# Self attention with its head mixing in two column halves and its value and score weights on two row halves

## The chip, the cores and the metric

The kernel runs on one core of a Trainium2 chip. The metric is the time of one execution on the device, in microseconds (us). TensorE (PE in the profile) multiplies matrices, VectorE (DVE), ScalarE (ACT) and GpSimd (POOL) work on elements, SyncE (SP) issues the transfers. Each engine runs its own instructions in order and waits on semaphores for the others.

## The reference

A perceiver block: cross attention, self attention and a feed forward part, each added to `x`, which has 64 sequences of 32 rows of 512. The change touches self attention alone:

```python
def _holo_linear(x, basis, phase, amp):
    resonance = jnp.einsum('bsd,hd->bsh', x, basis)      # 512 -> 64
    w = amp * jnp.cos(phase)                             # 512 x 64
    return jnp.einsum('bsh,oh->bso', resonance, w)
q = _holo_linear(hidden_states, basis_q, phase_q, amp_q)   # k and v alike
# 16 heads of 32
scores = jnp.einsum('bhqd,bhkd->bhqk', q, k) * scale
attn = jax.nn.softmax(scores, axis=-1)
out = jnp.einsum('bhqk,bhkd->bhqd', attn, v)
# heads side by side: 512
return _holo_linear(out, basis_o, phase_o, amp_o)
...
x = x + _L0_attn_ref(_layernorm(x, axis=-1), ...)
```

## The kernel before

`perceiver_block` runs one stage after another, each in a block of its own: `query_path`, `cross_attention`, `root_deviations`, `holo_weights`, `self_attention`, `root_deviations` again, `fold_weights` and `feed_forward`. A block ends when all engines are through it.

`holo_weights` loads amplitudes, phases and bases, forms amplitude times cosine and multiplies them into `score_w` (64 rows, per head 64 columns) and `value_w` (per head 64 columns, kept on partitions 64 to 127). `out_w` (64 rows of 512) are the output weights. The unused halves of `phase` and `amp` are cleared by VectorE (L1079, L1080), and SyncE waits for that ahead of the two loads of the output weights (L1069, L1072).

`self_attention` goes through 16 tiles of 128 rows, that is four sequences each. All data is fp32, for which TensorE executes each matmul as two passes; a transpose is one pass. A tile `t` takes these steps on TensorE, each with the engine that takes its result out of PSUM:

- `turn_input` (L1218): four transposes of the normalised rows, which GpSimd makes one to two tiles ahead (L1207, L1209); ScalarE copies them to `xn_t` (L1353).
- `reduce_input` (L1227): 8 matmuls with the bases; ScalarE copies `reduced` (L1362; queries' part on partitions 0 to 63, values' part on 64 to 127) and twice `keys` (L1365).
- `score_weights` (L1238): 8 matmuls of 128 columns, on rows 0 to 63; ScalarE copies one half to `u_sb` (L1377), VectorE the other (L1340).
- `score` (L1249): 8 matmuls of 64 columns. VectorE takes the peak (L1304) and subtracts it (L1306), ScalarE takes the exponential (L1385), VectorE sums (L1311), inverts (L1313) and scales (L1315).
- `turn_weights` (L1265): four transposes of the weights; VectorE and ScalarE copy two blocks each to the block-diagonal `e_t` (L1181).
- `value_weights` (L1257): 2 matmuls of 512 columns, on rows 64 to 127; VectorE (L1329) and ScalarE (L1357) copy half each to `z_sb`.
- `mix` (L1273): 16 matmuls, one for each head, with 64 stationary columns, all adding into one 64 x 128 area; ScalarE copies it to `ro_sb` (L1381).
- `project` (L1278): 1 matmul of 512 columns, on rows 0 to 63. VectorE adds it to the rows of `x` (L1322) and forms the negative mean (L1325), ScalarE sums the squares (L1370), VectorE stores both (L1335, L1336).

The order of the steps is written out by hand and spans three tiles. On TensorE a step of the loop is:

```python
turn_input(t, v); project(t - 2); value_weights(t - 1, 1 - v)
reduce_input(t, v); turn_weights(t - 1, 1 - v)
score_weights(t, v); mix(t - 1); score(t, v)
```

Queries for one tile are weighed while the tile before is mixed. Turned weights and projection share a PSUM bank (`P_BANK`), so `turn_weights` waits for VectorE's addition; the mix shares the bank of the reduction. SyncE issues the loads of `fold_weights` at the start of the stage (`loads.first`).

Elsewhere in the kernel, `reduce` of the query path (L432) writes alternating matmuls to two column halves:

```python
for ab in range(2):
    one = nc.tensor.matmul(ps[ab * R:(ab + 1) * R, QR_BANK, s * B:(s + 1) * B], m_sb[:, ab, sign, at * R:(at + 1) * R],
                           q_sb[:, ab, sign, s * B:(s + 1) * B], start=True, stop=True)
```

Of the kernel before, what the change touches and what calls it, by code (L numbers as in the profile page):

```python
# [1047 lines left out]
def holo_weights(nc, amp_nat, phase_nat, basis_t, basis_o, amp_o, phase_o, half_pi, basis, score_w, value_w, out_w):  # L1048
# [3 lines left out]
    with ExitStack() as ctx:  # L1052
# [8 lines left out]
        loaded, cleared, stepped, cosined, weighed, multiplied, kept = (  # L1061
            sem(f"h_{n}") for n in ("loaded", "cleared", "stepped", "cosined", "weighed", "multiplied", "kept"))
        block = ctx.enter_context(nc.Block())

        @block.sync
        def _(sp):
            sp.dma_start(phase[:, 0:NAT], phase_nat.rearrange("p t i -> p (t i)")).then_inc(loaded, 16)
            sp.wait_ge(cleared, 1)
            sp.dma_start(phase[0:HARM, NAT:], phase_o).then_inc(loaded, 16)  # L1069
            sp.dma_start(amp[:, 0:NAT], amp_nat.rearrange("p t i -> p (t i)")).then_inc(loaded, 16)  # L1070
            sp.wait_ge(cleared, 2)
            sp.dma_start(amp[0:HARM, NAT:], amp_o).then_inc(loaded, 16)  # L1072
            sp.dma_start(bo[:], basis_o).then_inc(loaded, 16)
            sp.dma_start(basis[:], basis_t).then_inc(loaded, 16)
            sp.wait_ge(loaded, 96)

        @block.vector
        def _(dve):
            nc.vector.memset(phase[:, NAT:], 0.0).then_inc(cleared, 1)  # L1079
            nc.vector.memset(amp[:, NAT:], 0.0).then_inc(cleared, 1)  # L1080
            dve.wait_ge(loaded, 96)
            dve.wait_ge(cleared, 2)
# [12 lines left out]
            nc.vector.tensor_copy(out_w[:], amp[0:HARM, NAT:])  # L1095
# [40 lines left out]
def self_attention(nc, x1, stat, basis, score_w, value_w, out_w, ident, loads):  # L1136
# [4 lines left out]

    with ExitStack() as ctx:
# [8 lines left out]
        shifted = sb("d_shifted", [P, 2, HH, S])  # L1151
# [4 lines left out]
        ro_sb = sb("d_ro", [HARM, P])  # L1156
# [27 lines left out]
        def in_steps(engine, step):  # L1184

            step(0, 0, mid=False, old=False)
            step(1, 1, old=False)
            with engine.Fori(1, TURNS) as i:
                step(2 * i, 0)
                step(2 * i + 1, 1)  # L1190
            step(TILES, 0, new=False)
            step(TILES + 1, 1, new=False, mid=False)
# [20 lines left out]
        def _(pe):  # L1213
# [7 lines left out]
            def reduce_input(t, v):  # L1221
                pe.wait_ge(turned_out, t + 1)
                wait(pe, reduced_out, t)
                wait(pe, ro_out, t - 1)
# [27 lines left out]

            def value_weights(t, v):
                wait(pe, z_out_a, t)
                wait(pe, z_out_d, t)
                for g in range(2):
                    last = nc.tensor.matmul(ps[:, Z_BANK + g], reduced[HARM:2 * HARM, v],  # L1257
                                            value_w[HARM:2 * HARM, 8 * g:8 * g + 8].rearrange("p h j -> p (h j)"), start=True, stop=True)
                last.then_inc(z_done, 1)
# [40 lines left out]
        def _(dve):  # L1300
            def shift(t, v):
# [4 lines left out]
                nc.vector.tensor_tensor(shifted[:, v], scores, peak[:, v].unsqueeze(2).to_broadcast([P, HH, S]),  # L1306
# [10 lines left out]
            def step(t, v, new=True, mid=True, old=True):  # L1317
                if mid:
                    weigh(t - 1, 1 - v)
                if old:  # L1320
                    dve.wait_ge(out_done, t - 1)
                    nc.vector.scalar_tensor_tensor(row_of(t - 2), ps[:, P_BANK], 1.0, row_of(t - 2), ALU.mult, ALU.add,  # L1322
                                                   accum_out=row_sum[:]).then_inc(added, 1)
                    dve.wait_ge(added, t - 1)
                    nc.vector.tensor_scalar(neg_mean[:], row_sum[:], -1.0 / D, None, ALU.mult).then_inc(centred, 1)  # L1325
                if mid:
                    dve.wait_ge(z_done, t)
                    wait(dve, ro_done, t - 1)
                    nc.vector.tensor_copy(z_sb[:, 0:8].rearrange("p h j -> p (h j)"), ps[:, Z_BANK]).then_inc(z_out_d, 1)  # L1329
                if mid:  # L1330
                    dve.wait_ge(e_turned, t)
                    copy_blocks("dve", (0, 1)).then_inc(e_out_d, 1)
                if old:
                    dve.wait_ge(squared, t - 1)
                    nc.vector.tensor_copy(stat[:, 0, bass.ds(t - 2, 1)], neg_mean[:])  # L1335
                    nc.vector.tensor_copy(stat[:, 1, bass.ds(t - 2, 1)], squares[:]).then_inc(kept, 1)  # L1336
                if new:
                    dve.wait_ge(u_done, t + 1)
                    wait(dve, scored, t)
                    nc.vector.tensor_copy(u_sb[:, 1], ps[:, U_BANK + 1].rearrange("p (k b s) -> p b k s", k=HG, b=BT)).then_inc(u_out_d, 1)  # L1340
                    shift(t, v)

            dve.sem_inc(kept, 1)
            dve.wait_ge(cleared, 1)
            in_steps(dve, step)

        @block.scalar
        def _(act):
            def step(t, v, new=True, mid=True, old=True):
                if new:  # L1350
                    act.wait_ge(turned, t + 1)
                    wait(act, reduced_done, t)
                    nc.scalar.activation(xn_t[:], ps[:, T_BANK].rearrange("p (c x) -> p c x", c=CD), ACT.Copy).then_inc(turned_out, 1)  # L1353
                if mid:
                    act.wait_ge(z_done, t)
                    wait(act, ro_done, t - 1)
                    nc.scalar.activation(z_sb[:, 8:16].rearrange("p h j -> p (h j)"), ps[:, Z_BANK + 1], ACT.Copy).then_inc(z_out_a, 1)  # L1357
                if new:
                    act.wait_ge(reduced_done, t + 1)
                    wait(act, scored, t - 1)  # L1360
                    wait(act, z_done, t - 1)
                    nc.scalar.activation(reduced[:, v], ps[:, R_BANK, 0:P], ACT.Copy)  # L1362
                    for parity in range(2):
                        at = slice(parity * HARM, (parity + 1) * HARM)
                        last_key = nc.scalar.activation(keys[at, v, :, parity], ps[at, R_BANK, P:2 * P].rearrange("p (b s) -> p b s", b=BT), ACT.Copy)  # L1365
                    last_key.then_inc(reduced_out, 1)
                if old:
                    act.wait_ge(centred, t - 1)
                    act.wait_ge(kept, t - 1)
                    nc.scalar.activation(scratch[:], row_of(t - 2), ACT.Square, bias=neg_mean[:], accum_out=squares[:]).then_inc(squared, 1)  # L1370
                if mid:
                    act.wait_ge(e_turned, t)
                    copy_blocks("act", (2, 3)).then_inc(e_out_a, 1)
                if new:
                    act.wait_ge(u_done, t + 1)
                    wait(act, scored, t)
                    nc.scalar.activation(u_sb[:, 0], ps[:, U_BANK].rearrange("p (k b s) -> p b k s", k=HG, b=BT), ACT.Copy).then_inc(u_out_a, 1)  # L1377
                if mid:
                    act.wait_ge(ro_done, t)
                    wait(act, out_done, t - 1)  # L1380
                    nc.scalar.activation(ro_sb[:], ps[0:HARM, R_BANK, 2 * P:3 * P], ACT.Copy).then_inc(ro_out, 1)  # L1381
                if new:
                    act.wait_ge(shifted_out, t + 1)
                    wait(act, e_turned, t - 1)
                    nc.scalar.activation(e[:, v], shifted[:, v], ACT.Exp).then_inc(exped, 1)  # L1385

            act.wait_ge(cleared, 2)
            in_steps(act, step)


# [498 lines left out]
def perceiver_block(nc, x, x_s, cache_t, early, w_qr, w_kr, late, angle_q, centre_q, rope_kv, amp_nat, phase_nat, basis_t, basis_o, amp_o, phase_o,  # L1889
# [4 lines left out]
    with ExitStack() as ctx:  # L1894
# [27 lines left out]
        with ExitStack() as fold_scope:  # L1922
            loads = FoldLoads(nc, fold_scope, paths, ent_in, ent_out, path, columns)
            with ExitStack() as scope:
                basis, score_w, value_w, out_w = (scope.enter_context(nc.sbuf_tensor(n, shape, F32)) for n, shape in (
                    ("basis", [P, CD, 2 * P]), ("score_w", [HARM, 16, HARM]), ("value_w", [P, 16, HARM]), ("out_w", [HARM, D])))
# [71 lines left out]
```

## Time and profile before

| | before |
|---|---|
| median of 3 runs | 1765.01 us (1761.34 to 1765.61) |
| the profiled execution | 1764.15 us, span 1762.3 us |
| TensorE busy | 1547.7 us (88%) |
| VectorE busy | 1127.6 us (64%) |
| ScalarE busy | 810.1 us (46%) |
| GpSimd busy | 542.6 us (31%) |
| granted TensorE clock, mean | 0.943 |

The span runs from the first to the last instruction. Busy times are sums of instructions, of which several of TensorE can overlap; a row of a timeline can merge several instructions of one kind (their number stands behind the x). The shape of a matmul is given as rows x columns of the stationary operand, then output and input. A granted clock of 1.00 is 2.4 GHz, 0.50 is 1.2 GHz.

### The profile page before, as it was taken

What the parts mean: (1) busy time and instruction counts of PE and PEld (TensorE: products, weight loads), DVE (VectorE), ACT (ScalarE), POOL (GpSimd) and SP (SyncE); (2) the same over time, 40 slices, a digit from 0 to 9 for tenths busy, and PEclk for the clock granted to TensorE, in tenths of its full rate; (3) what the DMA queues carried; (4) which work ended last, traced back from release to release, by engine and by line L of the source; (5) the groups of instructions that cost most, each with busy time, mean ns of one, the idle gap of its engine ahead of it and who ended that gap; (6) DMA issues with size and microseconds to landing.
All of it is one profiled execution on the core that took longest, in us unless ns stands there. A gap on an engine that the chain in (4) does not pass through costs nothing. (4 is left out here: it accounts for less than half of the span.)

```text
span 1762.3 us, 26302 instructions
## 1 busy us (share of the span) xinstructions
PE 1547.7 (88%) x8136; PEld 1171.3 (66%) x8136; DVE 1127.6 (64%) x1818; ACT 810.1 (46%) x1723; POOL 542.6 (31%) x594
## 2 busy tenths in 40 slices
PE   5899999999559999999999399999758679898996
PEld 4577777777347777777777277787423258686775
DVE  6888887777257788877777224544356625464646
ACT  4565656565335555555554223433201244555553
POOL 5233443230144545455553121110041030403102
PEclk9899999999789999999999679999889879999998
DMA  4143233333384444454442130000143100000000
GB/s 159 42 123 97 88 108 109 108 100 110 103 277 110 120 110 119 114 119 113 116 113 60 54 130 0 0 0 0 72 191 140 51 0 1 25 1 24 0 25 24
DMA packets 137878, 143.46 MB, mean 81 GB/s; under 512 B 83168, under 2 KB 102752, under 8 KB 134112
## 3 DMA queue, kind: packets, MB, share of 16 engines
q1 hardware_dynamic: 136096, 133.60, 25.9%
q10 hardware_dynamic: 1728, 9.20, 1.6%
q8 instruction: 27, 0.44, 0.1%
q14 instruction: 27, 0.22, 0.0%
HBM read 113.27 MB, written 29.49 MB: 81 GB/s over the span
## 5 line engine op out<-in xcount | busy, mean ns | idle before, releaser
L901 ACT ACTIVATE c_e_t_high<-c_et_ps 128x512 fp32r<-128x512 f32 x128 | 76.7, 599 | 226.3 <-PE c_et_ps L966 226.3
L77 DVE TENSOR_TENSOR b_rot_parts_low<-b_rot,b_rot_parts_high 128x1536 fp32r<-128x1536 f32 x64 | 136.3, 2130 | 22.3 <-ACT b_rot_parts_high L526 22.3
L794 POOL TENSOR_TENSOR c_mixed_low<-c_whole,c_mixed_high 128x512 fp32r<-128x512 f32 x64 | 95.3, 1490 | 176.0 <-ACT c_mixed_high L913 176.0
L958 PE MATMUL c_sc_ps<-c_kv_t,c_q 128*128 128x257 f32 x512 | 136.3, 390 | 13.7 <-DMA c_q<-carried_queries 13.7
L1500 PE MATMUL f_ps<-f_right,f_left 128*128 128x512 f32 x256 | 115.9, 615 | 27.9 <-DMA f_right<-ent_out 20.6
L817 DVE TENSOR_REDUCE c_peak<-c_sc_ps 128x2 f32<-128x514 f32 x128 | 88.6, 692 | 54.5 <-PE c_sc_ps L958 53.8
L70 PE MATMUL e_mm_ps<-folded_high,e_h_t_high 128*128 128x512 f32 x256 | 108.7, 425 | 15.8 <-DVE e_h_t_low L77 15.7
L958 PEld LDWEIGHTS c_sc_ps<-c_kv_t,c_q 128*128 128x128 f32 x512 | 99.4, 195 | 32.9 <-DMA c_q<-carried_queries 14.5
L264 POOL TENSOR_TENSOR b_turned_raw<-b_turn_part 128x384 f32<-128x384 f32 x32 | 68.9, 2155 | 164.9 <-DVE b_key_parts_low L77 163.6
L309 DVE TENSOR_TENSOR b_rot<-b_w_qr,b_angle 128x1536 f32<-128x1536 f32 x64 | 118.9, 1858 | 0.2
L893 ACT ACTIVATE c_e<-c_sc_ps,c_peak 128x257 f32<-128x257 f32 x256 | 118.8, 475 | 0.0
L966 PE MATMUL c_et_ps<-ident,c_e 128*128 128x128 f32 x512 | 82.5, 285 | 36.8 <-DVE c_e L824 35.0
L70 PE MATMUL b_ps<-b_x_t_high,b_wq_parts_high 128*128 128x512 f32 x256 | 108.2, 423 | 5.0 <-DVE b_x_t_low L77 5.0
L1500 PEld LDWEIGHTS f_ps<-f_right,f_left 128*128 128x128 f32 x256 | 50.2, 198 | 93.7 <-issue 65.6
L70 PE MATMUL c_out_ps<-c_w_vo_high,c_mixed_high 128*128 128x512 f32 x256 | 110.7, 432 | 1.6 <-POOL c_mixed_low L794 1.6
L77 DVE TENSOR_TENSOR c_e_t_low<-c_et_ps,c_e_t_high 128x512 fp32r<-128x512 f32 x128 | 88.0, 688 | 30.4 <-ACT c_e_t_high L901 30.4
L966 PEld LDWEIGHTS c_et_ps<-ident,c_e 128*128 128x128 f32 x512 | 59.9, 144 | 71.0 <-DVE c_e L824 64.8
L260 POOL TENSOR_TENSOR b_turn_part<-b_early,b_centre 128x384 f32<-128x384 f32 x64 | 84.9, 1346 | 71.9 <-DMA b_early<-early 70.2
L526 ACT ACTIVATE b_rot_parts_high<-b_rot 128x1536 fp32r<-128x1536 f32 x64 | 95.2, 1487 | 25.3 <-PE b_ps L72 17.0
L1684 POOL TENSOR_TENSOR e_y<-e_y,out_norm 128x512 f32<-128x512 f32 x16 | 22.5, 1406 | 263.7 <-DVE e_y L1844 263.7
L72 PE MATMUL e_mm_ps<-folded_high,e_h_t_low 128*128 128x512 f32 x256 | 103.5, 404 | 0.0
L71 PE MATMUL e_mm_ps<-folded_low,e_h_t_high 128*128 128x512 f32 x256 | 103.5, 404 | 0.0
(214 smaller groups left out, 4026.2 us busy)
## 6 DMA issues: line engine op xcount, KB each, us to landing
c_q<-carried_queries SPq DMA_DIRECT2D x64, 256.0 KB, 3.6
c_ends_spread<-end_weights SPq DMA_DIRECT2D x64, 256.0 KB, 4.3
carried_queries<-x SPq DMA_DIRECT2D x7, 2048.0 KB, 11.2
b_early<-early SPq DMA_DIRECT2D x15, 640.0 KB, 3.9
c_raw<-cache_t SPq DMA_DIRECT2D x64, 128.5 KB, 3.9
c_swapped<-cache_t SPq DMA_DIRECT2D x128, 64.2 KB, 3.8
f_left<-ent_in SPq DMA_DIRECT2D x8, 1024.0 KB, 5.1
f_right<-ent_out SPq DMA_DIRECT2D x8, 1024.0 KB, 7.8
```

What stands on the lines that cost most here:

```text
L70: nc.tensor.matmul(out, left[0], right[0], start=start, stop=False)
L71: nc.tensor.matmul(out, left[0], right[1], start=False, stop=False)
L72: return nc.tensor.matmul(out, left[1], right[0], start=False, stop=stop)
L77: return nc.vector.tensor_tensor(low, value, high.bitcast(F32), ALU.subtract)
L309: nc.vector.tensor_tensor(rot[:, k % 2], weight, angles, ALU.mult).then_inc(rot_ready, 1)
L526: nc.scalar.activation(rot_parts[0][:, k % 2], rot[:, k % 2], ACT.Copy).then_inc(rot_rounded, 1)
L794: nc.gpsimd.tensor_tensor(mixed[1][:, w, :, u], whole[:, u % 2].rearrange("p (h s) -> p h s", h=H), mixed[0][:, w, :, u].bitcast(F32), ALU ...
L817: nc.vector.tensor_reduce(peak[:, v], sc_ps[:, 2 * v:2 * v + 2, 0:L], AX_X, ALU.max, negate=True).then_inc(peaked, 1)
L893: last = nc.scalar.activation(e[:, v, c], sc_ps[:, 2 * v + c, 0:L], ACT.Exp, bias=peak[:, v, c:c + 1], accum_out=total[:, v, c:c + 1])
L958: last = nc.tensor.matmul(sc_ps[:, 2 * half + c, 0:L], q[:, u, at], kv_t[:, u], start=True, stop=True)
L966: last = nc.tensor.transpose(et_ps[:, (2 * k + c) * P:(2 * k + c + 1) * P], e[:, half, c, k * P:(k + 1) * P], ident[:])
L1500: last = nc.tensor.matmul(ps[:, m], left[:, slot, m * P:(m + 1) * P], right[:, slot], start=k == 0, stop=k == CF - 1)
```

## The change

- The mix writes even heads to partitions 0 to 63 and odd heads to 64 to 127 of `P_BANK`, as two sums. `ro_sb` gets 128 rows, and `out_w` holds its 64 rows twice, so that the projection over 128 rows adds the two sums. For this `amp_o` and `phase_o` are handed over with their rows doubled; the two memsets and the waits for them go.
- `score_weights` and `value_weights` become one step, `weigh_reduced`, of the tile itself: value matmul of a half, four score matmuls of the half, and the same for the other half.
- A step of the loop has a new order, on all engines. TensorE turns and reduces the input of the next tile in it, and projects in the same step in which it mixes. `score` waits for each half of `u_sb` by itself. `shifted` has one buffer in place of two. The loop is one step shorter.

```diff
-            nc.vector.memset(phase[:, NAT:], 0.0).then_inc(cleared, 1)
-            nc.vector.memset(amp[:, NAT:], 0.0).then_inc(cleared, 1)
...
-            nc.vector.tensor_copy(out_w[:], amp[0:HARM, NAT:])
+            nc.vector.tensor_copy(out_w[:], amp[:, NAT:])
...
-        ro_sb = sb("d_ro", [HARM, P])
+        ro_sb = sb("d_ro", [P, P])
...
-            def score_weights(t, v):
+            def weigh_reduced(t, v):
+
                 pe.wait_ge(reduced_out, t + 1)
                 wait(pe, u_out_a, t)
                 wait(pe, u_out_d, t)
+                wait(pe, z_out_a, t)
+                wait(pe, z_out_d, t)
                 for g in range(2):
+                    values = nc.tensor.matmul(ps[:, Z_BANK + g], reduced[HARM:2 * HARM, v],
+                                              value_w[HARM:2 * HARM, 8 * g:8 * g + 8].rearrange("p h j -> p (h j)"), start=True, stop=True)
                     for k in range(HG):
                         h = 8 * g + 2 * k
                         last = nc.tensor.matmul(ps[:, U_BANK + g, k * P:(k + 1) * P], score_w[:, h:h + 2].rearrange("p h j -> p (h j)"),
                                                 reduced[0:HARM, v], start=True, stop=True)
-                last.then_inc(u_done, 1)
+                    last.then_inc(u_done, 1)
+                    values.then_inc(z_done, 1)
...
             def score(t, v):
-                pe.wait_ge(u_out_a, t + 1)
-                pe.wait_ge(u_out_d, t + 1)
                 wait(pe, shifted_out, t)
                 out = ps[:, S_BANK].rearrange("p (g q b s) -> p g b q s", g=2, q=2, b=BT)
                 for g in range(2):
+                    pe.wait_ge(u_out_d if g else u_out_a, t + 1)
...
                 for h in range(HH):
-                    last = nc.tensor.matmul(ps[0:HARM, R_BANK, 2 * P:3 * P], z_sb[:, h], e_t[:, h], start=h == 0, stop=h == HH - 1)
-                last.then_inc(ro_done, 1)
+                    half = h % 2
+                    one = nc.tensor.matmul(ps[half * HARM:(half + 1) * HARM, P_BANK, 0:P], z_sb[:, h], e_t[:, h],
+                                           start=h < 2, stop=h >= HH - 2)
+                    if h >= HH - 2:
+                        one.then_inc(ro_done, 1)
...
-            def step(t, v, new=True, mid=True, old=True):
+            def step(t, v, new=True, mid=True, old=True, ahead=True):
                 if new:
-                    turn_input(t, v)
-                if old:
-                    project(t - 2)
-                if mid:
-                    value_weights(t - 1, 1 - v)
-                if new:
-                    reduce_input(t, v)
+                    weigh_reduced(t, v)
                 if mid:
                     turn_weights(t - 1, 1 - v)
                 if new:
-                    score_weights(t, v)
+                    score(t, v)
+                if ahead:
+                    turn_input(t + 1, 1 - v)
                 if mid:
                     mix(t - 1)
-                if new:
-                    score(t, v)
+                if ahead:
+                    reduce_input(t + 1, 1 - v)
+                if mid:
+                    project(t - 1)
+
+            turn_input(0, 0)
+            reduce_input(0, 0)
             in_steps(pe, step)
```

VectorE's order in a step is then: `add(t - 2)` (addition and mean), copy of the score weights' second half, its two blocks of `e_t`, `keep(t - 2)`, peak and shift of `t`, sum, inverse and scaling of `t`, copy of its half of `z_sb`. ScalarE's: copy of the score weights' first half, squares of `t - 2`, its two blocks of `e_t`, copy of the input of `t + 1`, exponential of `t`, copy of the mix of `t - 1`, its half of `z_sb`, `reduced` and `keys` of `t + 1`.

## Rows read from the trace of the kernel before

**Rows 1.** The page's first line
```profile
span 1762.3 us, 26302 instructions
```

**Rows 2.** Three stretches: length, busy PE, PEld, DVE, ACT, POOL, clock, DMA, GB/s
```profile
1014.00:1027.00 13.00, 10.26 (x44) 9.30 (x44) 0.69 (x1) 3.18 (x6) 4.26 (x5) 0.50 0.98 417
...
1126.00:1159.20 33.20, 31.46 (x230) 25.54 (x228) 18.73 (x41) 14.52 (x34) 6.25 (x6) 1.00 0.00 0
...
1231.00:1248.00 17.00, 10.33 (x45) 7.74 (x44) 7.04 (x18) 4.19 (x9) 0.00 (x0) 0.78 0.00 1
```

**Rows 3.** Timeline of TensorE, one step: start, duration, instruction, [idle before]
```profile
1125.23 0.60 PE L1218 MATMUL d_ps<-ident,d_xn 128*128 128x128 f32 x4
1125.76 0.69 PE L1278 MATMUL d_ps<-out_w,d_ro 64*128 64x512 f32 x1
1125.77 0.69 PE L1257 MATMUL d_ps<-value_w,d_reduced 64*128 64x512 f32 x1
1126.30 0.59 PE L1278 MATMUL d_ps<-out_w,d_ro 64*128 64x512 f32 x1
1126.30 1.45 PE L1257 MATMUL d_ps<-value_w,d_reduced 64*128 64x512 f32 x3
1128.05 2.05 PE L1227 MATMUL d_ps<-d_xn_t,basis 128*128 128x128 f32 x16 [0.30 <-ACT d_xn_t L1353]
1130.00 0.63 PE L1265 MATMUL d_ps<-ident,d_e 128*128 128x128 f32 x4
1130.90 2.05 PE L1238 MATMUL d_ps<-d_reduced,score_w 64*128 64x128 f32 x16 [0.28 <-ACT d_keys L1365]
1132.96 3.71 PE L1273 MATMUL d_ps<-d_e_t,d_z 128*64 128x128 f32 x32
1136.60 2.00 PE L1249 MATMUL d_ps<-d_keys,d_u 128*128 128x64 f32 x16
1138.43 0.61 PE L1218 MATMUL d_ps<-ident,d_xn 128*128 128x128 f32 x4
```

**Rows 4.** Timelines of VectorE and ScalarE in the same step
```profile
1125.43 0.69 DVE L1304 TENSOR_REDUCE d_peak<-d_ps 128x16 f32<-128x512 f32 x1 [4.95 <-PE d_ps L1249]
...
1128.55 0.69 DVE L1315 TENSOR_TENSOR d_e<-d_e,d_inverse 128x512 f32<-128x512 f32 x1
...
1130.66 1.38 DVE L1181 COPY d_e_t<-d_ps 32x512 f32<-32x512 f32 x2
...
1130.14 0.28 ACT L1362 ACTIVATE d_reduced<-d_ps 128x128 f32<-128x128 f32 x1 [1.65 <-PE d_ps L1227]
1130.31 0.54 ACT L1365 ACTIVATE d_keys<-d_ps 64x128 f32<-64x128 f32 x2
```

**Rows 5.** Timeline of TensorE in the query path, around one run of line 432
```profile
301.94 0.39 PE L71 MATMUL b_ps<-b_rot_parts_low,b_key_parts_high 128*128 128x512 f32 x1
302.17 0.39 PE L72 MATMUL b_ps<-b_rot_parts_high,b_key_parts_low 128*128 128x512 f32 x1
302.48 1.15 PE L432 MATMUL b_ps<-x 128*64 128x64 f32 x32
303.56 0.50 PE L70 MATMUL b_ps<-b_x_t_high,b_wq_parts_high 128*128 128x512 f32 x1
```

**Rows 6.** Timelines, stage's start, third turn of the input, last mix, last instruction
```profile
1014.23 1.11 PE L1218 MATMUL d_ps<-ident,d_xn 128*128 128x128 f32 x4 [6.17 <-POOL d_xn L1209]
...
1046.01 0.61 PE L1218 MATMUL d_ps<-ident,d_xn 128*128 128x128 f32 x4
...
1237.77 6.66 PE L1273 MATMUL d_ps<-d_e_t,d_z 128*64 128x128 f32 x32 [1.53 <-ACT d_e_t L1181]
...
1247.79 0.14 DVE L1336 COPY stat<-d_squares 128x1 f32<-128x1 f32 x1
```

**Rows 7.** Timeline of the preparation: first memset and second load
```profile
987.39 0.48 DVE L1079 MEMSET h_phase<- 128x512 f32 x1 [0.68 <-PEq L1025]
987.90 0.47 SPq L1069 DMA_DIRECT2D h_phase<-phase_o  x1
```

More of the change, by code:

```diff
@@ L1187, in in_steps @@
             step(1, 1, old=False)
-            with engine.Fori(1, TURNS) as i:
+            with engine.Fori(1, TURNS - 1) as i:
                 step(2 * i, 0)
                 step(2 * i + 1, 1)
-            step(TILES, 0, new=False)
-            step(TILES + 1, 1, new=False, mid=False)
+            step(TILES - 2, 0)
+            step(TILES - 1, 1, ahead=False)
+            step(TILES, 0, new=False, ahead=False)
         @block.sync
@@ L1223, in reduce_input @@
                 wait(pe, reduced_out, t)
-                wait(pe, ro_out, t - 1)
                 for m in range(2):
@@ L1251, in score @@
                 last.then_inc(scored, 1)
[L1253 to L1259, printed above, removed]
             def turn_weights(t, v):
@@ L1305, in shift @@
                 dve.wait_ge(peaked, t + 1)
-                nc.vector.tensor_tensor(shifted[:, v], scores, peak[:, v].unsqueeze(2).to_broadcast([P, HH, S]),
+                wait(dve, exped, t)
+                nc.vector.tensor_tensor(shifted[:], scores, peak[:, v].unsqueeze(2).to_broadcast([P, HH, S]),
                                         ALU.subtract).then_inc(shifted_out, 1)
@@ L1315, in weigh, with step @@
                 nc.vector.tensor_tensor(e[:, v], e[:, v], inverse[:, v].unsqueeze(2).to_broadcast([P, HH, S]), ALU.mult).then_inc(weighed, 1)
-            def step(t, v, new=True, mid=True, old=True):
-                if mid:
-                    weigh(t - 1, 1 - v)
+            def step(t, v, new=True, mid=True, old=True, ahead=True):
                 if old:
[L1321 to L1329, printed above, removed]
+                    add(t - 2)
+                if new:
+                    dve.wait_ge(u_done, 2 * t + 2)
+                    wait(dve, scored, t)
+                    nc.vector.tensor_copy(u_sb[:, 1], ps[:, U_BANK + 1].rearrange("p (k b s) -> p b k s", k=HG, b=BT)).then_inc(u_out_d, 1)
@@ L1343, in _, with keep @@
+            def keep(t):
+                dve.wait_ge(squared, t + 1)
+                nc.vector.tensor_copy(stat[:, 0, bass.ds(t, 1)], neg_mean[:])
+                nc.vector.tensor_copy(stat[:, 1, bass.ds(t, 1)], squares[:]).then_inc(kept, 1)
             dve.sem_inc(kept, 1)
@@ L1345, in _ @@
             in_steps(dve, step)
+            add(TILES - 1)
+            keep(TILES - 1)
         @block.scalar
         def _(act):
-            def step(t, v, new=True, mid=True, old=True):
-                if new:
[L1351 to L1366, printed above, removed]
@@ new lines, in take_input, with take_reduced @@
+            def take_input(t):
+                act.wait_ge(turned, t + 1)
+                wait(act, reduced_done, t)
+                nc.scalar.activation(xn_t[:], ps[:, T_BANK].rearrange("p (c x) -> p c x", c=CD), ACT.Copy).then_inc(turned_out, 1)
+            def take_reduced(t, v):
+                act.wait_ge(reduced_done, t + 1)
+                wait(act, scored, t - 1)
+                nc.scalar.activation(reduced[:, v], ps[:, R_BANK, 0:P], ACT.Copy)
+                for parity in range(2):
+                    at = slice(parity * HARM, (parity + 1) * HARM)
+                    last_key = nc.scalar.activation(keys[at, v, :, parity], ps[at, R_BANK, P:2 * P].rearrange("p (b s) -> p b s", b=BT), ACT.Copy)
+                last_key.then_inc(reduced_out, 1)
@@ new lines, in square, with step @@
+            def square(t):
+                act.wait_ge(centred, t + 1)
+                act.wait_ge(kept, t + 1)
+                nc.scalar.activation(scratch[:], row_of(t), ACT.Square, bias=neg_mean[:], accum_out=squares[:]).then_inc(squared, 1)
+            def step(t, v, new=True, mid=True, old=True, ahead=True):
+                if new:
+                    act.wait_ge(u_done, 2 * t + 1)
+                    wait(act, scored, t)
+                    nc.scalar.activation(u_sb[:, 0], ps[:, U_BANK].rearrange("p (k b s) -> p b k s", k=HG, b=BT), ACT.Copy).then_inc(u_out_a, 1)
@@ L1367, in step @@
                 if old:
-                    act.wait_ge(centred, t - 1)
-                    act.wait_ge(kept, t - 1)
-                    nc.scalar.activation(scratch[:], row_of(t - 2), ACT.Square, bias=neg_mean[:], accum_out=squares[:]).then_inc(squared, 1)
+                    square(t - 2)
                 if mid:
                     act.wait_ge(e_turned, t)
+                    wait(act, ro_done, 2 * t - 2)
                     copy_blocks("act", (2, 3)).then_inc(e_out_a, 1)
[L1374 to L1381, printed above, removed]
+                if ahead:
+                    take_input(t + 1)
                 if new:
@@ L1384, in step @@
                     wait(act, e_turned, t - 1)
-                    nc.scalar.activation(e[:, v], shifted[:, v], ACT.Exp).then_inc(exped, 1)
+                    nc.scalar.activation(e[:, v], shifted[:], ACT.Exp).then_inc(exped, 1)
+                if mid:
+                    act.wait_ge(ro_done, 2 * t)
+                    wait(act, out_done, t - 1)
+                    nc.scalar.activation(ro_sb[:], ps[:, P_BANK, 0:P], ACT.Copy).then_inc(ro_out, 1)
+                if new:
+                    act.wait_ge(z_done, 2 * t + 2)
+                    wait(act, ro_done, 2 * t)
+                    nc.scalar.activation(z_sb[:, 8:16].rearrange("p h j -> p (h j)"), ps[:, Z_BANK + 1], ACT.Copy).then_inc(z_out_a, 1)
+                if ahead:
+                    take_reduced(t + 1, 1 - v)
             act.wait_ge(cleared, 2)
+            take_input(0)
+            take_reduced(0, 0)
             in_steps(act, step)
+            square(TILES - 1)
 LAYERS, PW, QUARTERS = 2, 2, 4
```

35 lines of the change are left out of this document (19 added, 16 removed).

## The prediction

> **What bounds the kernel now.** I read the page first: the profiled execution spans 1762.3 us [rows 1] and took 1764.15 us, 1.85 us more outside the span, and so lies 0.9 us under the median of 1765.01 us. The change touches two stages, so I cut the span by time. Self attention issues its first TensorE instruction at 1014.2 us and its last VectorE instruction ends at 1247.9 us [rows 6]: 233.7 us, 13% of the span, for 16 tiles. In the busy times by stretch the reader is to see that TensorE works 31.5 of 33.2 us in the middle, VectorE 18.7, ScalarE 14.5 and GpSimd 6.3, at the full granted clock [rows 2]. So TensorE bounds the stage, and what counts is the start-to-start time of its groups.
>
> The timeline of TensorE over one step gives these [rows 3]. From one turn of the input (1125.23) to the next (1138.43) are 13.20 us: turn of the input 0.53; projection and value weights up to the reduction 2.29, of which 0.30 is waiting for ScalarE; reduction 1.95; turn of the weights 0.90, of which 0.28 is waiting for the keys; score weights 2.06; mix 3.64; scores 1.83. Two kinds of rate stand in it. The mix is 32 passes (an fp32 matmul is two) in 3.64 us, 114 ns a pass. The scores are 16 passes of half as many columns, and also 114 ns each.
>
> **The change part by part, per step.**
>
> *Mix in two column halves.* The same 32 passes go, but even heads write partitions 0 to 63 and odd heads 64 to 127. The stage of before has no such pair, but line 432 of the query path has: 32 passes, 64 stationary columns, full 128 rows, output alternating between the two halves. It takes 1.08 us from its start to the next group's start [rows 5], some 0.1 us of which is the change of shape (its first pass starts 0.31 us after the matmul ahead of it, where such matmuls follow each other at 0.23). That is 31 ns a pass for 64 columns. If the mix's 114 ns at 128 columns stands for streaming, 64 columns take 57 ns; the halves therefore overlap completely there. Bounds for the mix: 3.64 us (no overlap) and 32 x 57 ns = 1.82 us; I take 1.82 + 0.10 = 1.92, by the nearest row. Gain 1.72.
> The Trainium skill, page "TensorE: Matmul & The Clock Gate", Part 3, says that a weight load overlaps a running matmul only when the row groups differ. Here both halves use all rows, so by it each pass would pay its load too, and the mix would keep a good part of its 3.64 us. Line 432 has the same shape and ran at 31 ns a pass, so the trace does not agree, and I go by the row.
>
> *Value and score weights on two row halves.* Value weights (4 passes of 512, rows 64 to 127) now go in between the score weights (16 passes of 128, rows 0 to 63): value group, eight score passes, value group, eight score passes. Today the value weights hide the projection in the same way: the first value pass starts 0.01 us after the first projection pass and 0.53 us before the second one [rows 3]. A pass of 512 takes 0.43 us (three in 1.45, the end of the last included), and the six passes need 1.99 us (1125.76 to 1127.75), not 2.6. So row halves overlap, and a pass of one half goes ahead of a waiting pass of the other. Alone the score weights take 2.06 and the four value passes 4 x 0.43 = 1.72. Bounds: 2.06 (shorter wholly inside longer) and 3.78 (one after the other). I take 2.06: the pattern is that of the projection and value pair, only with unequal lengths.
> The same part of that page states that matmuls start strictly in program order. By it the first score pass would start with the second value pass, 0.43 us late, twice a step; that is the in-order rival below. The value pass that starts before the second projection pass [rows 3] speaks against it.
>
> *Projection.* With both column halves of the mix as 128 rows and the output weights doubled, it is again two passes of 512, but on all rows, so nothing lies beside it: 2 x 0.43 = 0.86. It is moved behind the reduction, where it covers ScalarE's copies of reduced and keys. Today from the reduction's end (1130.00) to the score weights (1130.90) are 0.90 us: ScalarE starts at 1130.14, its last key copy ends at 1130.85 [rows 4]. So reduction to next step costs the larger of 0.86 and 0.90: 0.90. Without this cover the cost would be 0.86 + 0.90.
>
> *Sum.* Weights 2.06 + turn of the weights 0.55 + scores 1.83 + turn of the input 0.54 + mix 1.92 + reduction 1.95 + 0.90 = 9.75 us, against 13.20: 3.45 us a step.
>
> *Are the other engines early enough?* Count from the start of the value/score weights. ScalarE's copy of the first half of the score weights starts near 1.0 us, when eight passes are through; VectorE's of the second near 2.1, and ends at 2.8; the second half of the scores wants it at 3.5. The turned weights are there at 2.6; VectorE's two copies of 0.69 end at 4.2, ScalarE's before that; the mix starts at 4.97, as the turn of the input stands ahead of it. Scores end at 4.43. From there VectorE takes 0.20 to start and 3.8 more through peak, shift, exp, sum and scaling (1125.43 to 1129.24, [rows 4]); shift waits for nothing, since exp of the tile before is long over. ScalarE's copy of the turned input (4.97 to 5.7) is over when exp comes, near 6.1. The weights are ready near 8.5 and turned at 11.9 in the next step: 3.4 us to spare. ScalarE copies the mix near 7.0; the projection starts at 8.85. The addition for the tile before follows the projection (9.9 to 10.7), and the next turn of the weights waits for it at 11.9: 1.2 us to spare, the narrowest. VectorE is busy 18.7 and ScalarE 14.5 us in 33.2 us [rows 2], which is 7.4 and 5.8 a step, both under 9.75. GpSimd's two operations are done one tile ahead. No wait but the 0.04 in the 0.90 should be left.
>
> *Head.* In the first 24 us the granted clock is half (0.50 in 1014 to 1027, [rows 2]) and a turn of the input takes 1.11 instead of 0.60 us [rows 3, 6]. I leave the clock as it was, full from 1038 on. By the doubled terms the new order runs: input turned and reduced 14.2 to 20.7 with ScalarE, weights(0) to 24.5, scores(0) to 28.2, turn(1), 0.75 of waiting, reduction(1) to 33.7, 0.9, weights(1) to 38.3, then at full clock the rest of step 1, 8.1 us: step 2 begins at 1046.4. Today step 2 begins at 1046.0 [rows 6], so nothing is gained here: the reduction and turn of tile 2 already lie behind.
> *Middle.* 13 steps: 13 x 13.20 = 171.6 becomes 13 x 9.75 = 126.8, to 1173.2.
> *Tail.* Today 1217.6 to 1247.9, 30.3 us. New: the last full step ends with project(14) at 7.7 us; VectorE then finishes weights(15), the z copy and the addition at 9.9; turn 0.6, copies 1.5, mix 1.9, copy 0.4, projection 1.0, addition, square and store 2.1 make 17.4. TensorE has gaps of some 2 us here; today in such gaps the clock fell and the last mix took 6.66 instead of 3.71 us [rows 3, 6], so I add 1.6: 19.0. The end is at 1192.2 instead of 1247.9: 55.7 us less.
>
> *Preparation.* Two memsets go. Today the second load is issued at 987.90, right behind the end of the first memset (987.39 + 0.48, [rows 7]); it can go at once. In return two loads have 128 rows, not 64. That is at best the 0.48 of a memset gained, and I allow as much lost; I take 0. The copy of the output weights has more partitions, not more elements in each. All after the stage is moved, not changed.
>
> Sum: 1764.15 - 55.7 = 1708.5, and with the 0.9 to the median 1709.4; I say 1710.
>
> **Rivals.**
> *In-order starts.* Score passes wait for the second value pass: 0.43 + eight passes (0.91), twice, is 2.7 us, with the 0.2 of the two changes of shape 2.85 instead of 2.06. 0.8 x 16 = 12.6: 1722. With no row overlap at all 3.78, 1.72 x 16 = 27.5: 1737. For: today's pair has equal lengths, an unequal pair is nowhere in the trace.
> *Column halves don't pay.* The mix stays at 3.64: 1.72 x 16: 1737. Against it is line 432 alone. If neither overlap comes, the step is 9.75 + 1.72 + 1.72 = 13.19 us: no change, 1765. That is the rival that the change does not do what it says.
> *A new wait.* The 1.2 us of the addition or the ScalarE chain (input copy, exp, mix copy, z copy, reduced) goes by 1 us: 10.7 a step, 1725.
> *Slower: the clock.* If TensorE, with 3.5 us less streaming a step, is held at half clock, its terms grow as the last mix did (6.66 against 3.71, by 1.8): 8.85 x 1.8 + 0.9 = 16.8, 7.1 more a step. It decides against the change when more than 3.45 / 7.1, about half of the steps, run so; with all of them 1710 + 114 = 1824. Against: the clock was full throughout with 0.58 us of waiting in each step, and less is left. A later rise at the start costs 0.45 us for each us.
>
> **How the numbers follow.** Chances: the forecast 0.62 (its own range 1703 to 1719: 9.4 to 10.2 us a step and the clock's rise up to 6 us later), in-order or no row overlap 0.15, new wait 0.10, column halves 0.05, neither 0.04, clock 0.04. 1700 to 1733 takes in the first three but for their far ends. 0.3% is 5.3 us, about what a measurement tells from no change: faster 0.92, same 0.04, slower 0.04.
>
> **What would show it.** Mix 1.9 us from start to next group, starts of the two halves together; value and score passes mixed in time, 2.1 us; projection behind the reduction with under 0.1 us idle; turns of the input 9.75 us apart; the granted clock 1.00. Wrong would be: score passes that start 0.43 us late, gaps ahead of the turn of the weights with VectorE's addition as releaser, or half clock.

## The result, and the profile after

| | before | after |
|---|---|---|
| median | 1765.31 us (4 runs) | 1702.02 us (4 runs, 1701.08 to 1703.14) |
| ratio | | 0.9646, 95% interval 0.9629 to 0.9663 |
| self attention, first turn of the input to last store | 233.7 us | 170.6 us |
| a step in the middle | 13.20 us | 9.50 us |

63 us less, where 55 were forecast (1710); the range of 1700 to 1733 holds it. All of it lies in self attention: outside of the stage the profiled executions take 1528.6 us before and 1528.7 us after. One of the six executions of the kernel with neither edit (below) took 3657 us, twice as long as its others, and is left out of its numbers. The page of the kernel after, its first lines:

```profile
span 1699.3 us, 26369 instructions
## 1 busy us (share of the span) xinstructions
PE 1490.1 (88%) x8136; PEld 1129.8 (66%) x8136; DVE 1126.8 (66%) x1816; ACT 809.9 (48%) x1723; POOL 540.8 (32%) x594
```

Not one pass fewer (8136), and still less TensorE time: the busy time is no sum, as the section on the time before has it, but counts overlapping instructions once (below, 123.60 us of 123.60). The timeline of TensorE over one step (after), beside [rows 3]:

```profile
1109.77 0.69 PE L1235 MATMUL d_ps<-value_w,d_reduced 64*128 64x512 f32 x1
1109.77 0.71 PE L1239 MATMUL d_ps<-d_reduced,score_w 64*128 64x128 f32 x4
1110.30 0.59 PE L1235 MATMUL d_ps<-value_w,d_reduced 64*128 64x512 f32 x1
1110.32 0.61 PE L1239 MATMUL d_ps<-d_reduced,score_w 64*128 64x128 f32 x4
...
1111.16 0.59 PE L1235 MATMUL d_ps<-value_w,d_reduced 64*128 64x512 f32 x1
1111.21 0.61 PE L1239 MATMUL d_ps<-d_reduced,score_w 64*128 64x128 f32 x4
1111.75 0.66 PE L1258 MATMUL d_ps<-ident,d_e 128*128 128x128 f32 x4
1112.24 1.90 PE L1250 MATMUL d_ps<-d_keys,d_u 128*128 128x64 f32 x16
1113.98 0.61 PE L1215 MATMUL d_ps<-ident,d_xn 128*128 128x128 f32 x4
1114.52 1.97 PE L1267 MATMUL d_ps<-d_e_t,d_z 128*64 128x128 f32 x32
1116.41 2.05 PE L1223 MATMUL d_ps<-d_xn_t,basis 128*128 128x128 f32 x16
1118.30 1.02 PE L1274 MATMUL d_ps<-out_w,d_ro 128*128 128x512 f32 x2
1119.27 0.69 PE L1235 MATMUL d_ps<-value_w,d_reduced 64*128 64x512 f32 x1
```

Each value pass has four score passes beside it, and the 32 passes of the mix take 1.89 us, 59 ns each in place of 114. The mean of a pass, 59 ns, includes the start of the group. No row carries an idle time. Start to start, in us:

| group | forecast | measured |
|---|---|---|
| value and score weights | 2.06 | 1.98 |
| turn of the weights | 0.55 | 0.49 |
| scores | 1.83 | 1.74 |
| turn of the input | 0.54 | 0.54 |
| mix | 1.92 | 1.89 |
| reduction | 1.95 | 1.89 |
| projection, to the next step | 0.90 | 0.97 |
| step | 9.75 | 9.50 |

The rest of the surplus is in the head. Busy times by stretch (after): length, then PE, PEld, DVE, ACT, POOL, the granted clock, share and rate of DMA:

```profile
1024.00:1026.00 2.00, 2.00 (x14) 1.78 (x10) 0.00 (x0) 0.60 (x1) 0.00 (x0) 0.50 1.04 446
1026.00:1028.00 2.00, 2.00 (x17) 2.00 (x17) 0.69 (x1) 0.00 (x0) 0.00 (x0) 0.89 1.03 442
...
1031.30:1033.70 2.40, 0.04 (x1) 0.00 (x0) 2.23 (x4) 0.96 (x4) 0.00 (x0) 1.00 0.00 0
...
1043.20:1166.80 123.60, 123.60 (x1225) 107.53 (x1224) 87.02 (x182) 67.24 (x156) 22.89 (x22) 1.00 0.00 0
```

The clock became full 10.7 us after the stage's start (1015.75), not 25 us as before, and TensorE was busy for all of the 13 steps in the middle. One new wait stands at 1031.3, and the last mix ran at the low clock again (3.68 us in place of 1.97). TensorE's rows of the second tile's weights and of the last mix, and the last store (after):

```profile
1033.74 0.66 PE L1235 MATMUL d_ps<-value_w,d_reduced 64*128 64x512 f32 x1 [2.40 <-DVE d_z L1333]
...
1178.92 3.68 PE L1267 MATMUL d_ps<-d_e_t,d_z 128*64 128x128 f32 x32 [1.51 <-ACT d_e_t L1177]
...
1186.20 0.14 DVE L1345 COPY stat<-d_squares 128x1 f32<-128x1 f32 x1
```

By parts: the head (to the third step's start, 1043.24) took 27.5 us, forecast 32.2; the middle 123.5, forecast 126.8; the tail 19.6, forecast 19.0. That is 170.6 in place of 178.0.

### The profile page after: what moved, and what is told of

The parts are those of the page before. It is cut to its first block and busy times, and to the rows that moved or that the text cites. A ratio compares the mean times of both kernels' runs of the same rounds, so it can differ in the third digit from the quotient of the medians.

```text
span 1699.3 us, 26369 instructions
## 1 busy us (share of the span) xinstructions
PE 1490.1 (88%) x8136; PEld 1129.8 (66%) x8136; DVE 1126.8 (66%) x1816; ACT 809.9 (48%) x1723; POOL 540.8 (32%) x594
## 6 DMA issues: line engine op xcount, KB each, us to landing
carried_queries<-x SPq DMA_DIRECT2D x7, 2048.0 KB, 11.2
```

## The experiments

Every kernel was compared with the kernel before in the same job; ratios have 95% intervals. "Step" is the start-to-start time in the middle of the stage. The changed kernel, once more in the last job, gave 1701.72 us, 0.9644 (0.9631 to 0.9658).

**One column half.** The mix writes partitions 0 to 63 alone.

```diff
-                    half = h % 2
-                    one = nc.tensor.matmul(ps[half * HARM:(half + 1) * HARM, P_BANK, 0:P], z_sb[:, h], e_t[:, h],
-                                           start=h < 2, stop=h >= HH - 2)
+                    one = nc.tensor.matmul(ps[0:HARM, P_BANK, 0:P], z_sb[:, h], e_t[:, h],
+                                           start=h == 0, stop=h == HH - 1)
```

> The changed kernel with all 16 heads of the mix in one column half (the other half of the copied sum is zero). Theory (column halves overlap completely): the mix goes back from 1.89 to about 3.64 us, every other group of TensorE stays, so the step goes from 9.50 to 11.25 us and the time from 1702 by 16 x 1.75 to about 1730 us. Rival (the new order is what gave the time, the halves gave little): under 1710 us.

1729.42 us, 0.9794 (0.9772 to 0.9817). Timeline of TensorE:

```profile
1108.09 3.71 PE L1267 MATMUL d_ps<-d_e_t,d_z 128*64 128x128 f32 x32
1111.73 2.05 PE L1224 MATMUL d_ps<-d_xn_t,basis 128*128 128x128 f32 x16
```

The mix takes 3.64 us again, as in [rows 3], and the step 11.25. The column halves give 1.75 us a step, where the forecast had 1.72.

**Values by themselves.** `value_w`'s matmuls leave `weigh_reduced` and follow `score`.

```diff
                 if new:
                     score(t, v)
+                    weigh_values(t, v)
```

> The changed kernel with the value weights as a group of their own behind the scores, where no work on the other row half stands next to them. Theory (row halves overlap): score weights alone keep their 2.0 us, four value passes of 0.43 us and one or two changes of shape come on top, 1.75 to 1.95 us, so a step of about 11.35 us and 1731 us. Rival (the values would hide as well elsewhere, or ScalarE and VectorE bound the step): step under 10 us, under 1710.

1742.68 us, 0.9869 (0.9852 to 0.9885), slower than expected by 12. Timeline of TensorE, one step:

```profile
1100.99 1.98 PE L1243 MATMUL d_ps<-value_w,d_reduced 64*128 64x512 f32 x4
1102.91 0.66 PE L1215 MATMUL d_ps<-ident,d_xn 128*128 128x128 f32 x4
...
1108.25 2.05 PE L1237 MATMUL d_ps<-d_reduced,score_w 64*128 64x128 f32 x16
1110.23 0.65 PE L1260 MATMUL d_ps<-ident,d_e 128*128 128x128 f32 x4
...
1112.54 1.98 PE L1243 MATMUL d_ps<-value_w,d_reduced 64*128 64x512 f32 x4
```

The values cost 1.91 us, the score weights stay at 1.98, the step is 11.55: the row halves give 2.05 us, not 1.72. Of the 0.33 more, 0.19 are in the values' own group (4 x 0.43 = 1.72) and 0.14 in the scores and the turn of the input beside it (1.83 and 0.59 us, not 1.74 and 0.54): a group next to one of another shape takes some 0.1 us longer. 2.05 x 16 = 33 explains four fifths of the 41 us to the changed kernel. The rest lies in the head. The profiled execution was the longest of the four (1749.16 us), but 6 of its 48 us over the changed kernel lie outside the stage; in the stage it takes 42 us more, 15 of them in the head, as busy times by stretch of this kernel tell, whose stage starts at 1020.0:

```profile
1052.00:1056.00 4.00, 4.00 (x6) 0.50 0.00 0
1056.00:1060.00 4.00, 4.00 (x43) 0.75 0.00 0
```

Here the clock was at half for 38 us of the stage.

**Neither.** Both edits together.

> Both undone, the new order of steps kept. Theory (all of the gain is the two overlaps, the order only keeps the engines fed): step of 9.50 + 1.75 + 1.85 = 13.1 us, against 13.20 before, and 1759 us. Rival (the order alone has a gain, by fewer waits): 12.6 us a step and 1752; or the order alone loses: over 1765.

1770.40 us (five executions), 1.0030 (1.0015 to 1.0044): 0.3% slower than the kernel before, where 1759 was expected. The step is 13.29 us, 3.79 more than in the changed kernel, and the two edits cost 1.75 and 2.05 one by one: they add. The new order alone gains nothing in the middle (13.20 before). It saves the waits of [rows 3], 0.30 and 0.28, but the projection no longer lies beside the values (1.91 + 0.97 us in place of 1.99). Here too the low clock lasted for some 41 us at the head, and the head takes 8 us more than before (45.3 against 37.5, to the third tile's score weights), which the expectation left out.

**Column halves in the old order.** The kernel before, with the mix in halves and the doubled output weights.

```diff
-                    last = nc.tensor.matmul(ps[0:HARM, R_BANK, 2 * P:3 * P], z_sb[:, h], e_t[:, h], start=h == 0, stop=h == HH - 1)
+                    half = h % 2
+                    one = nc.tensor.matmul(ps[half * HARM:(half + 1) * HARM, R_BANK, 2 * P:3 * P], z_sb[:, h], e_t[:, h],
+                                           start=h < 2, stop=h >= HH - 2)
```

> The kernel before, with the mix in two column halves and the doubled output weights as only change. Theory: the mix falls by 1.75 us a step, but the projection over all 128 rows no longer lies beside the value weights (4 x 0.43 + 2 x 0.43 = 2.6 instead of 1.99, and a change of shape of 0.1), so a step of about 12.15 us and 1748 us. Rival (the full gain of the mix arrives): 11.45 us and 1737. Rival (the old order's waits eat it): no change.

1744.31 us, 0.9884 (0.9868 to 0.9901), steps of 11.95 and 12.09 in turn, 12.02 on average. Timeline of TensorE:

```profile
1102.38 1.02 PE L1276 MATMUL d_ps<-out_w,d_ro 128*128 128x512 f32 x2
1103.34 1.98 PE L1252 MATMUL d_ps<-value_w,d_reduced 64*128 64x512 f32 x4
1105.25 2.05 PE L1222 MATMUL d_ps<-d_xn_t,basis 128*128 128x128 f32 x16
...
1110.16 1.97 PE L1269 MATMUL d_ps<-d_e_t,d_z 128*64 128x128 f32 x32
```

The mix is short at once, but the projection stands by itself for 0.96 us where [rows 3] show it beside the values. A third of the mix's gain (1.18 of 1.74 is left) is lost until the projection gets another use.

**How far does TensorE look ahead?** Two kernels keep all halves but don't alternate them.

```diff
-                    half = h % 2
+                    half = h // 8
```

> The changed kernel with heads 0 to 7 in the first column half and 8 to 15 in the second, so the two halves come one behind the other and not in turn. Theory (a pass can start ahead of a few waiting passes of the other half, not of 14): the halves overlap only around their border, mix about 3.5 us, step 11.1 us, 1728. Rival (TensorE looks ahead as far as it likes): mix 1.9 us, 1702.

In the second, the two value matmuls follow all score weights.

```diff
                 for g in range(2):
-                    values = nc.tensor.matmul(ps[:, Z_BANK + g], reduced[HARM:2 * HARM, v],
...
                     last.then_inc(u_done, 1)
-                    values.then_inc(z_done, 1)
+                for g in range(2):
+                    nc.tensor.matmul(ps[:, Z_BANK + g], reduced[HARM:2 * HARM, v],
...
```

> The changed kernel with all 16 score passes first and the 4 value passes behind them, no other edit. Theory (look ahead of a few passes): the value passes start when nearly all score passes are through, weights 1.98 + 1.5 = 3.5 us, step 11.0 us, 1727. Rival (look ahead without limit): the first value pass starts with the first score pass, step 9.5 us, 1702.

1722.22 us, 0.9772 (0.9755 to 0.9789), and 1725.16, 0.9794 (0.9768 to 0.9820). Timelines of TensorE, first the blocks, then the values last:

```profile
1110.94 3.33 PE L1267 MATMUL d_ps<-d_e_t,d_z 128*64 128x128 f32 x32
1114.20 1.05 PE L1223 MATMUL d_ps<-d_xn_t,basis 128*128 128x128 f32 x7
```

```profile
1102.86 1.71 PE L1237 MATMUL d_ps<-d_reduced,score_w 64*128 64x128 f32 x13
1104.30 0.69 PE L1241 MATMUL d_ps<-value_w,d_reduced 64*128 64x512 f32 x1
1104.41 0.49 PE L1237 MATMUL d_ps<-d_reduced,score_w 64*128 64x128 f32 x3
1104.84 1.45 PE L1241 MATMUL d_ps<-value_w,d_reduced 64*128 64x512 f32 x3
```

The reader sees the first value pass start ahead of exactly three of the 16 score passes. It is so in each of the seven steps looked at. The blocks' mix takes 3.26 us, 0.38 less than with one half, again three passes (3 x 0.114 = 0.34): pass by pass, the first one of the second half starts 0.006 us after the 13th of the first half's 16. So a pass went ahead of three waiting ones here, and halves overlap only if they alternate that closely in the program.

**Projection ahead of the reduction.**

```diff
+                if mid:
+                    project(t - 1)
                 if ahead:
                     reduce_input(t + 1, 1 - v)
-                if mid:
-                    project(t - 1)
```

> The changed kernel with the projection ahead of the reduction. Theory: it waits for the copy of the mix (0.45 us) and no longer covers the copies of reduced and keys (0.95 us instead of 0), so 1.4 us a step: 10.9 us, 1724. Rival (the place of the projection does not matter, other waits shrink in exchange): under 1708.

1718.89 us, 0.9744 (0.9725 to 0.9763). Timeline of TensorE:

```profile
1105.78 1.13 PE L1274 MATMUL d_ps<-out_w,d_ro 128*128 128x512 f32 x2 [0.40 <-ACT d_ro L1394]
1106.74 1.95 PE L1223 MATMUL d_ps<-d_xn_t,basis 128*128 128x128 f32 x16
1109.50 0.69 PE L1235 MATMUL d_ps<-value_w,d_reduced 64*128 64x512 f32 x1 [0.81 <-ACT d_keys L1366]
```

Both covers gone, two waits, step 10.84 and not 9.50: the place behind the reduction is worth 1.34 us a step.

**The new wait in the head.** VectorE copies its half of the values ahead of the weighing, and a dummy exponential loads ScalarE's table early.

```diff
                     wait(dve, ro_done, 2 * t)
-                    weigh(t, v)
                     nc.vector.tensor_copy(z_sb[:, 0:8].rearrange("p h j -> p (h j)"), ps[:, Z_BANK]).then_inc(z_out_d, 1)
+                    weigh(t, v)
...
             act.wait_ge(cleared, 2)
+            nc.scalar.activation(scratch[:, 0:1], ident[:, 0:1], ACT.Exp)
             take_input(0)
```

> The changed kernel with VectorE's copy of the value weights ahead of sum, inverse and scaling, and ScalarE's table for the exponential loaded at the start of the stage. Theory: in the steady steps nothing changes (9.50 us), as the turned weights have 2.9 us to spare; in the first step the wait for that copy (2.40 us) and the table load (1.28 us) go, 2.3 us less in all: 1699.7. Rival (the later weights hold TensorE up): step over 9.6 us, over 1704.

1697.02 us, 0.9626 (0.9610 to 0.9643). The second tile's weights (timeline of TensorE):

```profile
1032.68 0.69 PE L1235 MATMUL d_ps<-value_w,d_reduced 64*128 64x512 f32 x1 [0.81 <-ACT d_keys L1366]
```

The 2.40 us of waiting for `d_z` are 0.81 for the keys, which is 1.6 us gained in the head, and the step stays at 9.50. The stage takes 168.2 us (1016.3 to 1184.5), 2.4 less, but the other 0.8 us lie in the tail (18.7 against 19.6 us), and the unchanged kernel, profiled again below, has a tail of 18.9. So 1.6 of the expected 2.3 us are shown. The interval overlaps that of the changed kernel; the times alone show no gain. The two edits were not tried one by one: the table's load (1.28 us) stood in the same chain as the copy, and either of them alone may bring most of it.

**The clock at the head.** The changed kernel again, and two with idle matmuls ahead of the stage.

```diff
+            for _ in range(48):
+                nc.tensor.matmul(ps[:, 0, 0:P], ident[:], ident[:], start=True, stop=True)
             pe.wait_ge(weighed, 1)
...
+            for _ in range(20):
+                nc.tensor.matmul(ps[:, P_BANK, 0:P], ident[:], ident[:], start=True, stop=True)
             turn_input(0, 0)
```

> The changed kernel word for word, once more. It shows how much of the head of the stage is chance: in the first profile the clock was full 10.5 us after the stage's first matmul, before the change 24.5 us after it. Theory (the instant wanders from execution to execution): it is full at another time, anywhere from 5 to 40 us after, and the time is 1702 within 3 us, by 0.46 us for each us. Rival (the new order makes it rise early): 10 to 12 us again.

> The changed kernel with TensorE kept busy ahead of the stage: 48 fp32 matmuls of 128 x 128 x 128 with the identity in the preparation while it waits for the loads, 20 more at the start of self attention, whose results nobody reads. Theory (the low clock at the head costs 0.46 us for each us of it, and comes from TensorE's idle time in the preparation): full clock from the stage's start, 10.5 us of low clock less, 4.5 to 5 us: 1697. Rival (the head waits for ScalarE and VectorE anyway): the clock is full and the time stays at 1702. Rival (the extra matmuls hold up the first real ones): over 1704.

> The busy TensorE of e10_warm together with the earlier copy and table of e8_copy_first_table_early. Theory (both gains are of different waits and add): 1697 - 2.5 to 4 us, 1692 to 1695, the fastest of all. Rival (with a faster head the same wait bounds both): as the better of the two alone.

The changed kernel, profiled again, gives this row of the second tile's weights:

```profile
1034.34 1.19 PE L1235 MATMUL d_ps<-value_w,d_reduced 64*128 64x512 f32 x1 [2.40 <-DVE d_z L1333]
```

The clock rose 11.2 us after the stage's start, as the rival had it. But it fell again at 1034.1, 18.0 us into the stage, while TensorE waited for `d_z` (from 1031.9 to 1034.3), and was full for good only from 21.5 us on: the pass takes 1.19 us here, 0.66 in the first profile, which has the same wait and kept its clock. The head took 29.3 us, not 27.5, with the same program. So part of the head is chance, and theory and rival were each half right; the medians (1702.02 and 1701.72) don't differ. The busy one: 1702.86 us, 0.9644 (0.9628 to 0.9659); with the copy ahead too: 1698.89, 0.9630 (0.9616 to 0.9643). Timeline of TensorE in the former:

```profile
1006.42 0.81 PE L1122 MATMUL h_ps<-h_amp 32*64 32x64 f32 x20 [6.02 <-DVE h_amp L1088]
...
1007.24 1.01 PE L1128 MATMUL h_ps<-h_bo,h_amp 32*64 32x64 f32 x23
1010.02 7.30 PE L1295 MATMUL d_ps<-ident 128*128 128x128 f32 x40 [1.77 <-PEq L1052]
1017.15 0.60 PE L1217 MATMUL d_ps<-ident,d_xn 128*128 128x128 f32 x4
```

The clock is full at the first turn of the input (0.60 us, not 1.11 as in [rows 6]) and for the whole head. But the clock had fallen once more, at 1005.2, in the 6 us that TensorE waited inside the preparation, so that the 20 matmuls ran mostly at half clock and held the first turn up: in [rows 6] it follows the preparation's last matmul (until 1008.06) by 6.2 us, here (until 1008.25) by 8.9. In the profiled execution with both edits the stage takes 164.6 us, counted from its first turn as always, which starts late here too (8.8 us behind the preparation); the medians show no gain over either alone, where 1692 to 1695 was expected. The expectation of 1697 for the first was missed; 2.7 us of the gain went into the late start, and where the rest is, with a spread between executions of 1697.9 to 1703.1, stays open.

**How much room VectorE has.**

```diff
                 if old:
                     add(t - 2)
+                for n in range(3):
+                    nc.vector.tensor_tensor(spare[:], basis[:, 0:2].rearrange("p c x -> p (c x)"), basis[:, 0:2].rearrange("p c x -> p (c x)"), ALU.mult).then_inc(spared, 1)
+                    dve.wait_ge(spared, 3 * t + n + 1)
```

> The changed kernel with three extra VectorE products of 128 x 512 (0.72 us each, 2.15 us a step) between the addition and its copy of the score weights; nobody reads them. Theory (VectorE has 1.0 us of idle time there, and behind it 0.5 us until the second half of the scores wants the copy): 2.15 - 1.0 - 0.55 = 0.6 us a step, 10.1 us, with the last step 1712. Rival (VectorE bounds the step already): 2.15 us a step and 1736. Rival (it has far more room): 1702 to 1705.

1713.80 us, 0.9717 (0.9702 to 0.9731), step 10.34. Timelines, VectorE's copy for the scores and TensorE's second half of them:

```profile
1107.37 0.69 DVE L1326 COPY d_u<-d_ps 128x512 f32<-128x512 f32 x1 [0.21 <-DVE d_spare L1321]
...
1108.12 1.11 PE L1252 MATMUL d_ps<-d_keys,d_u 128*128 128x64 f32 x8 [0.64 <-DVE d_u L1326]
```

Of 2.15 us, 0.84 reach the step, where 0.6 was expected. The rest is room, and the wait that comes first is the one for `d_u`.

## Why the prediction was right

**The time.** 1702.0 lies in the range, but 1 us under the forecast's own 1703 to 1719: that allowed for a clock that rises later, not for one that rises earlier. The stage was to take 178.0 us and took 170.6. Of the 7.4 us, 4.7 are in the head and 3.3 in the middle, and the tail took 0.6 more.

**The bound.** TensorE's start-to-start times add up to the step before and after; with three more VectorE operations the step grows by less than half of their time. Right.

**Mix.** 1.92 forecast, 1.89 measured, and 3.64 with one half. Line 432 [rows 5] was the right row to go by: it alternates its halves in the same way. That this is a condition, the blocks show and the prediction did not say; that row and change share it was luck in this respect.

**Value and score weights.** 2.06 forecast, 1.98 measured. The in-order rival is refuted in its form: the first score pass starts with the first value pass, and four score passes start before the second value pass, which stands ahead of them in the program. But order counts at a longer distance: three passes. The page "TensorE: Matmul & The Clock Gate" of the Trainium skill (Part 3) has starts strictly in program order; the three score passes that start after the first value pass, though they stand ahead of it in the program, disagree.

**Projection.** 0.90 forecast, 0.97 measured, without idle time; with the cover gone 1.34 more. The forecast took 0.86 for its two passes and left out its own change of shape.

**Small terms.** Turn of the weights, scores and reduction were each taken 0.06 to 0.09 too long. The scores and the reduction were read where a wait or a change of shape stood beside them [rows 3], which the new order has not; the turn of the weights is 0.62 without its wait in [rows 3], and no row gives the 0.55 that was put for it. With the weights' 0.08 and the mix's 0.03, less the projection's 0.07, that is the 0.25 a step, 3.3 us over the middle.

**Room.** "1.2 us to spare, the narrowest" was wrong, without effect on the time: the copy of the score weights' second half was named with 0.7 us to spare (ends at 2.8, wanted at 3.5; the trace has 0.5), and it is what held TensorE up when VectorE was loaded.

**Preparation.** Nothing forecast, nothing measured: from the issue of the first load to the stage's first turn of the input are 27.0 us before and 26.9 after.

**Head.** This term was mis-sized: "I leave the clock as it was, full from 1038 on" gave 32.2 us, and it took 27.5. 0.4 us of it is a slip: the rest of step 1 is 9.75 - 2.06 = 7.7, not 8.1. The clock was full 10.7 us into the stage, not 23.8; at the forecast's 0.45 us for each us the 13.1 us are 5.9. The unforecast wait for `d_z` took back 1.6 (2.40 less the 0.81 for the keys). That makes 31.8 - 5.9 + 1.6 = 27.5. That the clock rose early was luck, of which the second profile of the same kernel had 1.8 us less.

What makes the clock rise is not settled. In the eight profiles that keep the value weights next to the score weights, the busied kernels left out, it first rose 5 to 11 us into the stage, but in five of them it fell once more and was full for good after 20 to 29 us. In the old order with column halves it rose after 6 us, fell, and was full for good after 23. In the other three kernels with the value weights as a group of their own it rose only after 25 (before), 38 and 41 us. That goes together in part, but no experiment changed that alone.

**Tail.** 19.0 forecast, 19.6 measured, with the last mix at half clock (3.68 us) as assumed.

## What to carry to other kernels

Matmuls that use half of the array's rows or columns overlapped here with those on the other half where they alternate in the program; issued in blocks they overlapped over three passes only. A part freed of half its time can expose its neighbour (the projection): plan a new place for it, behind a group whose result another engine still copies. Head and tail of a pipelined stage have waits and a clock of their own, and held more of the error here (4.7 and 0.6 us) than all steps of the middle (3.3).

## What was not expected of the hardware

TensorE lets a pass start ahead of waiting passes for another part of the array, so that it does not run its own instructions strictly in order, as the section on the chip has it. It was three passes in both trials: 13 of 16 score passes started before the first value pass, and the mix in blocks gained 0.38 us, about 3 x 0.114. Why three stays open. The granted clock stayed at half for 38 us in one kernel (values by themselves) and 10.7 in another (the changed one) that execute the same matmuls in another order, with TensorE busy for most of both stretches (35.0 of 38.1 us and 9.1 of 10.7).
